# A graph-attention kernel whose gathers may run at most four blocks ahead of VectorE's product

## The reference

```python
src = concatenate([src0, arange(n)]); dst = concatenate([dst0, arange(n)])   # every node also attends to itself
scores = einsum("ehd,ehd->eh", q[dst], k[src]) * scale                       # 8 heads of 32
m  = segment_max(scores, dst); ex = exp(scores - m[dst])
z  = segment_sum(ex, dst);     attn = ex / z[dst]
agg = segment_sum(attn[:, :, None] * v[src], dst)
h = h + agg.reshape(n, 256) @ wo + bo
h = h + gelu(layernorm(h) @ w1 + b1) @ w2 + b2
```

## Time and profile before

| | |
|---|---|
| runs, median (lowest to highest) | 3872.09 us (3860.8 to 3874.86) |
| the profiled execution, its own time | 3861.7 us |
| its span | 3859.9 us |
| mean granted TensorE clock | 0.735 |
| busy: VectorE / TensorE / POOL / ScalarE | 64% / 59% / 48% / 34% |
| edge part, first to last product of a layer | 251.0 us on in layer 0; 3302.7 us is the last of layer 1 |
| HBM | 161 GB/s over the span, about 205 GB/s in the edge parts |

### The profile page before, as it was taken

One profiled execution on the slowest core, in us unless ns is written; L12 is line 12 of the kernel. 1 busy time (PEld: TensorE's weight loads), 2 busy tenths in 40 slices (PEclk: granted clock), 3 DMA queues, 4 the chain that ended last, 5 costly groups with the idle time before them and its releaser, 6 DMA issues. The chain is left out here.

```text
span 3859.9 us, 35539 instructions
## 1 busy us (share of the span) xinstructions
PE 2259.6 (59%) x7207; PEld 1532.8 (40%) x7208; DVE 2485.9 (64%) x3966; ACT 1328.6 (34%) x3895; POOL 1842.0 (48%) x1938
## 2 busy tenths in 40 slices
PE   5634555455555555488854555555545555587897
PEld 3422333333333333366632333333333333365676
DVE  5766777777677777534435776876777777544333
ACT  1223444444443444122213443443444434222231
POOL 4055666666666665111036666666666666121000
PEclk8866766766676676699975666676667667689899
DMA  3365766666667666321246666666666667322101
GB/s 104 110 178 166 209 208 207 208 205 215 196 207 216 201 208 192 96 68 60 81 130 181 206 208 209 205 208 209 203 208 206 202 211 214 90 60 62 47 31 34
DMA packets 246235, 623.21 MB, mean 161 GB/s; under 512 B 46779, under 2 KB 102259, under 8 KB 246074
## 3 DMA queue, kind: packets, MB, share of 16 engines
q0 software_dynamic: 149904, 471.38, 41.1%
q1 hardware_dynamic: 96170, 150.25, 11.9%
HBM read 526.62 MB, written 94.78 MB: 161 GB/s over the span
## 5 line engine op out<-in xcount | busy, mean ns | idle before, releaser
L774 POOL DMA_INDIRECT ring<-kv_table,stage_ix x1760 | 1679.7, 954 | 1005.0 <-issue 554.0
L1020 PE MATMUL bank<-qs,hot_q 128*128 x1760 | 717.1, 556 | 706.1 <-issue 424.4
L1033 PE MATMUL bank<-ring,hot_w 128*128 128x272 f32 x1760 | 689.2, 530 | 501.7 <-issue 306.1
L1940 DVE TENSOR_TENSOR ring<-ring,bank 128x1024 f32<-128x1024 f32 x440 | 532.3, 1210 | 548.4 <-issue 359.1
L1020 PEld LDWEIGHTS bank<-qs,hot_q 128*128 128x128 f32 x1760 | 464.5, 276 | 886.7 <-issue 790.3
L1033 PEld LDWEIGHTS bank<-ring,hot_w 128*128 128x128 f32 x1760 | 412.7, 254 | 757.5 <-issue 497.5
L1945 DVE TENSOR_REDUCE s<-ring 128x32 f32<-128x1024 f32 x440 | 532.6, 1210 | 4.2
L1274 ACT ACTIVATE stage_o<-bank 128x272 f32<-128x272 f32 x440 | 167.5, 385 | 525.0 <-remote 318.3
L1258 ACT ACTIVATE s<-bank 128x8 f32<-128x8 f32 x440 | 78.1, 178 | 736.5 <-remote 434.8
L1248 ACT ACTIVATE hot_q<-pos_b,row_of 128x128 f32<-128x128 bf16 x880 | 303.8, 394 | 12.6 <-DMA pos_b<-rel_d 8.9
L1957 DVE TENSOR_TENSOR bank<-ring,bank 128x512 f32<-128x512 f32 x440 | 300.6, 683 | 0.0
(11 more groups left out here) (326 smaller groups left out, 2155.7 us busy)
## 6 DMA issues: line engine op xcount, KB each, us to landing
agg_d<-stage_o SPq DMA_DIRECT2D x108, 544.0 KB
ring<-kv_table,stage_ix POOLq DMA_INDIRECT x1760
pos_b<-rel_d SPq DMA_DIRECT2D x54, 256.0 KB
kv_table<-ring SPq DMA_DIRECT2D x50, 250.0 KB
h_dram<-ring SPq DMA_DIRECT2D x15, 625.0 KB
ring<-h_dram SPq DMA_DIRECT2D x15, 625.0 KB
ring<-in_x_dram SPq DMA_DIRECT2D x10, 625.0 KB
ring<-kv_table SPq DMA_DIRECT2D x10, 625.0 KB
```

The source lines that it names most:

```text
L774: gps.indirect_dma_start(out=chunk[:, par * G + i, j, :], out_offset=None, in_=table, in_offset=bass.IndirectOffsetOnAxis(ap=stage_ix[:, p ...
L1020: mm = ten.matmul(q_bank(third, i)[:, 0:QC], hot_q[:, i % 4, a * P:(a + 1) * P], qs[:, bass.ds(t * QC + a * QC, QC)], start=(a == 0), stop ...
L1033: mm = ten.matmul(b_acc[i % 2][:, lo - OWN:MC], hot_w[:, i % 4, :], chunk[:, s, j, lo:ROW], start=(j == 0), stop=(j == QD // 2 - 1), skip_ ...
L1940: tt(k_, k_, q, ALU.mult).then_inc(S["q_used"], 1)
```

## The change

Before the gathers of a block POOL now also waits until VectorE has done the product of the block four back in the same layer (`q_used` counts the products, 220 a layer). Blocks 0 to 3 of a layer have no such wait. The wait for the freed place stays, behind the new one.

```diff
+LEAD = 4
 ...
                     for i in range(n):
 ...
+                        if begin and par * G + i >= LEAD:
+                            pool.wait_ge(S["q_used"], layer * NB + par * G + i - LEAD + 1)
                         if not begin:
+                            hold(pool, S["q_used"], k * G + (layer * NB + i - LEAD + 1), S["pool_passed"])
                             hold(pool, S["agg"], (k - 2) * G + (layer * NB + i + 1), S["pool_passed"])
                         for j in range(QD):
                             gps.indirect_dma_start(out=chunk[:, par * G + i, j, :], ...)
```

## The result

The changed kernel takes **4011.27 us** (median of four runs, 4008.64 to 4018.86) against 3870.17 us for the kernel before (four runs on the same chip). The ratio is **1.0376**, 95% interval 1.0358 to 1.0394: slower by 3.8%. The forecast was 3976 us, 2.7% slower.

A forecast was written before the change was run, and what follows sets the result against it. Bound: 40.1 us of gathers a group plus stops where the stream must run dry for TensorE's late counts. 52 x 2.5 = +130, starts -18, sum +112 on 3861.7; with run offset, 3976 us; range 3770 to 4080 (own 3885 to 4040).

The forecast's parts named there:

- The waits' own instructions: On POOL, 216 added waits a layer, costed at nothing; 32 us if each showed at a quarter of the usual gap.
- Data would not be late: At VectorE's products, gathered data lands before it is needed, 15.6 us after the gather's release; cost zero.
- Two stops stay: In each steady group POOL still stops twice; a group grows from 47.1 to 49.6 us, +130 us over 52 groups.
- Stop A: POOL's 4.4 us stop each group, ending at 775.19 in the old profile; now ends through copy and product, +1.0 us.
- the bunch: TensorE's remaining late counts, arriving together once the gather stream is empty, up to 1.2 us later.
- Stop B: POOL's 3.1 us stop each group, ending at 793.15 in the old profile; predicted +1.5 us, bounds 0 and +2.2.
- the second rival: Three stops a group, or one mid softmax step; each more stop 5.3 us, 4250 us in all; chance 0.05.
- the starts: Start of each layer: POOL stops sooner, counts come 8 to 10 us earlier; together -18 us, between -30 and 0.
- One stop instead of two: First rival: the stream runs dry on its own in time, groups of 45.4 us, 3756 us; chance 0.20.
- Nothing moves: Third rival: steady groups stay as before, 3862 to 3872 us, or about 3850 with the starts' gain; chance 0.15.
- The signs: Expected in the profile after: POOL idle charged to VectorE's product, 5 us stops, groups about 49.6 us, GB/s down some 5%.

The follow-up runs named there:

- e4: Kernel before, with POOL also waiting before blocks 1 and 6 of each group until the previous block's gathers have landed; ratio 1.0011 to the kernel before.
- e5: Changed kernel, but POOL waits for ScalarE's copy of the block four back, not VectorE's product; ratio 0.9993 to the kernel before, on the 3434.34 us chip.
- e8: Kernel before, with gathers from each layer's third group fetching 1 KB rows instead of 2 KB; one run, 3430.42 us against 3434.34 us.
- e6: Changed kernel with a lead of five blocks instead of four; ratio 0.9998 to the kernel before, which takes 3434.34 us there.
- e3: Changed kernel with a lead of six blocks instead of four, at the start and in the loop; ratio 0.9965 to the kernel before.
- e10: The edit of e5 to the changed kernel, run on a chip with late counts; ratio 0.9960 to the kernel before, 3842.99 us there.
- e12: Changed kernel, with POOL waiting for ScalarE's copy at blocks 4 to 7 and for VectorE's product at blocks 0 to 3; ratio 0.9997 to the kernel before.
- e11: Kernel before, without TensorE's own count at its 220 waits a layer ahead of the queries, on a chip with late counts; ratio 0.9997 to the kernel before.

## Why the prediction was right, and what was too small in it

**What bounds the kernel.** Confirmed for this kind of chip: every version in which POOL does not wait for product 0 four blocks on comes out at 46.8 to 47.6 us a group, e4 puts most late copies at the dry moments, and where counts are on time the stops are gone and a group is the 40.1 us of gathers. That it is the stream that makes the counts late rests on their going together, and on e4. The rule of the Trainium skill ("SBUF — State Buffer", section "Who interferes with whom": DMA contends with no compute engine) was no guide to the time: a steady stream and late counts go together in every trace from the chips on which the kernel before takes 3843 to 3870 us. On the chip of e5 to e8 nothing speaks against the rule.

**The waits' own instructions** at nothing: right. e5 and e6 have them all and stay within 0.1% of before; so has e3, which is 0.35% faster.

**Data would not be late:** right. VectorE's long waits after the change are for copies and for a scan's count, not for gathers.

**Two stops stay:** right. Stop A as put (the bunch, copy, product, then POOL), at +1.0: the rows give 6.05 - 4.40 = +1.65. What was missing is the way of the product's count to POOL, 1.0 us, where I let the gather start at the product's end.

**Stop B is the step that failed.** I took +1.5 with +2.2 as the upper bound; the rows give 6.17 - 3.08 = +3.1. The prediction named the case ("it can also fall on the softmax step") and put it aside, with two reasons. One was that POOL's buffer of issued blocks hides it. It hides VectorE's wait, not POOL's own, and it is POOL that sets the pace. The other, in the second rival, was that the scans have their counts in steady groups. They had them because of where the old stops fell; the change moved the stops, and with them the lateness onto the scan. A third thing is missing: the prediction asked only at the two old stops whether the new wait binds, and rows 3 and 4 show that it binds at block 4 between them (gathers from 775.19 + 5.0 = 780.2, product 0 done at 784.1). e10 and e12 show that the wait behind product 0 and its neighbours is the loss. How much of it is the late scan and how much the lead itself is not separated by a run.

**The sum.** In place of 52 x 2.5 = +130, the 48 groups gave +170.4 (3.55 each: 5.0 in 31 of them, 0.9 in 17) and the tails +11.7; the starts -23.3 instead of -18; outside -9.3 instead of 0. That makes 149.5. So 3.55 us a group is above the upper bound of 1.0 + 2.2 = 3.2 that I had given, and it was luck that the time stayed inside the range: 17 groups hardly changed, and the starts and the parts outside gave back 33 us.

**The rivals.** One stop instead of two (3756): wrong, there are two in both layers. A stop in the middle of the softmax step (4250): its place was right, its price not. It is no third stop but the second one moved, and costs 1.6 us over what I gave stop B, not 5.3. Nothing moves: wrong here, right on the kind of chip where counts are on time (for the edits of e5 and e6; the changed kernel itself was not run there).

**The signs.** POOL's idle time went to the product (455.9 us); stops of 6.1 us, not 5; idle time before a product 9.67 where 7 or more was said; GB/s down 9% in the slower groups, not 5; the first scan of layer 1 waits 20.82 us, between the 18 that was said and the 25.6 of before; the parts outside changed by 1.2, 4.3 and 3.8 us.

## What to carry to other kernels

Before a producer is made to wait for a consumer, look at what else stands in the consumer's queue ahead of the instruction whose count is taken: here the same four blocks of lead cost 2.6 to 3.8% behind VectorE's product and nothing behind ScalarE's copy of the same block. In the old profile compare, for every block and not only at the stops, the start of the producer's work with the end of the instruction it is to wait for: here block 4's gathers ran 5.3 us ahead of product 0's end. A wait that is satisfied in the old profile, as the scan's was, is so for the old phases; when the change moves the stops, ask which wait they now fall on. And time a change on more than one chip where the profile shows counts that come long after their work: on one chip the two variants that were run (e5 and e6) were free.

## What the runs showed of the hardware

- The same kernel took 3843 to 3870 us (medians) in four sessions and 3434 us in one on another chip. Nearly the whole difference lies in the edge parts (423 of 430 us between the profiles of the kernel before and of e5, first to last product): a group takes 47.1 us on those and 40.1 on this, with equal durations of gathers and products.
- Where it is slow, TensorE's counts reach the other engines late while indirect gathers stream. In the profile of the kernel before, of the copies before which ScalarE was idle for over 0.5 us, the median from the end of the query's matmuls to the copy is 0.04 us for copies in the first 9 us of a stream (about 70), 5 us at 9 to 15 us (15), 12 at 15 to 20 (13), 13 at 20 to 25 (34). At the start of layer 1 one comes every 10.5 us, and the rest mostly when the queue is empty. What makes them late, and why not on the other chip, stays open: leaving out 220 of TensorE's own updates a layer changed nothing (e11), and whether shorter rows change it was measured only on the chip that does not have it (e8).
- Making POOL wait for the landing of its last gather costs a stop of 3.7 to 3.9 us (the medians of e4's two), though the queue is empty 2.2 to 2.4 us after the last issue.
- Of the versions tried, the wait for the copy (e10) is the fastest against before, 0.4%, and the lead of six (e3) 0.35%; both keep the gain at the start of layer 0 (98.9 and 96.0 us for the first 16 products, against 110.0), and little or none of that of layer 1 (111.9 and 114.1, against 113.9).
